# A graph layer on one core: nodes laid out 49 to a partition, and the prologue rearranged

## The reference

```python
h = maximum(layernorm(x), 0)
deg = maximum(zeros(n).at[dst].add(1.0), 1.0)
edge_weight = (deg[src] * deg[dst]) ** -0.5
edge_msg = relu(edge_attr @ W1e + b1e) @ W2e + b2e
messages = (h[src] + edge_msg) * edge_weight[:, None]
agg = segment_sum(messages, dst, n)
combined = (1.0 + gin_eps) * h + agg
out = relu(combined @ W1n + b1n) @ W2n + b2n + h
out = out * rsqrt(mean(out * out, -1) + RMS_EPS) * rms_w
return x + out
```

## Time and profile before

| | us |
|---|---|
| median of 3 runs | 1261.17 (1260.37 to 1263.86) |
| the profiled execution | 1260.41 |
| its span in the profile | 1257.8 |
| prologue, up to the first instruction of the edge pass | 0 to 122.5 |
| edge pass, up to the first instruction of the epilogue | 122.5 to 1182.5 |
| epilogue | 1182.5 to 1257.8 |

### The profile page before, as it was taken

One profiled execution on the slowest core, in us unless ns is written; L12 is line 12 of the kernel. 1 busy time (PEld: TensorE's weight loads), 2 busy tenths in 40 slices (PEclk: granted clock), 3 DMA queues, 4 the chain that ended last, 5 costly groups with the idle time before them and its releaser, 6 DMA issues. The chain is left out here.

```text
span 1257.8 us, 34843 instructions
## 1 busy us (share of the span) xinstructions
PE 1062.9 (85%) x12091; PEld 760.6 (60%) x12091; DVE 927.2 (74%) x4458; ACT 700.9 (56%) x1205; POOL 843.4 (67%) x849
## 2 busy tenths in 40 slices
PE   1041799999999999998999999999999989999475
PEld 0041477776666676666766666666676666666343
DVE  2996988787776787777867767777777678674266
ACT  1322566666565566655655656656666556565064
POOL 5221777777777777777777777777777777777012
PEclk9999999999999999999999999999999999999698
DMA  6007643533534434435435345344353353343442
GB/s 172 1 8 120 199 130 110 166 111 111 166 111 115 161 112 148 129 110 160 116 112 165 111 112 165 111 141 136 110 166 112 109 166 111 113 143 53 113 134 68
DMA packets 74824, 154.28 MB, mean 123 GB/s; under 512 B 22124, under 2 KB 48256, under 8 KB 68896
## 3 DMA queue, kind: packets, MB, share of 16 engines
q1 hardware_dynamic: 42372, 95.34, 22.2%
q0 software_dynamic: 25920, 53.55, 18.6%
q10 hardware_dynamic: 6364, 3.20, 1.0%
HBM read 145.38 MB, written 6.63 MB: 121 GB/s over the span
## 5 line engine op out<-in xcount | busy, mean ns | idle before, releaser
L863 POOL DMA_INDIRECT arena<-node_rows,arena x810 | 792.4, 978 | 267.0 <-issue 238.0
L1022 ACT ACTIVATE arena<-bank 128x686 f16<-128x686 f32 x405 | 367.9, 908 | 250.8 <-PE bank L934 250.5
L1014 ACT ACTIVATE arena<-bank 128x512 f32<-128x512 f32 (+1 forms) x450 | 245.2, 555 | 163.9 <-PE bank L889 122.4
L945 PE MATMUL bank<-t_words,arena 128*126 128x256 f16 x2205 | 299.5, 276 | 0.0
L889 PE MATMUL bank<-w1e,arena 64*128 64x128 f32 x3240 | 248.4, 273 | 0.0
L1104 DVE SCALAR_TENSOR_TENSOR arena<-iota_h,hi_f,bank 128x98 f32<-128x98 f32 x810 | 221.7, 310 | 27.0 <-PE bank L899 23.7
L945 PEld LDWEIGHTS bank<-t_words,arena 128*126 128x126 f16 x2205 | 235.3, 137 | 3.7 <-issue 2.9
L1088 DVE TENSOR_SCALAR arena<-iota_c,code 128x343 f16<-128x343 f16 x810 | 225.5, 320 | 6.1 <-PE bank L934 6.0
L889 PEld LDWEIGHTS bank<-w1e,arena 64*128 64x128 f32 x3240 | 217.6, 191 | 0.0
L1134 DVE TENSOR_TENSOR arena<-arena 128x128 f32<-128x128 f32 (+1 forms) x225 | 62.0, 275 | 172.4 <-DMA arena<-node_rows,arena 172.2
L934 PE MATMUL bank<-arena 128*128 128x343 f16 x810 | 186.2, 312 | 0.6 <-DVE arena L1088 0.2
(11 more groups left out here) (189 smaller groups left out, 882.3 us busy)
## 6 DMA issues: line engine op xcount, KB each, us to landing
arena<-in_attr SPq DMA_DIRECT2D x45, 1152.0 KB
arena<-low_src SPq DMA_DIRECT2D x45, 576.0 KB
arena<-node_rows,arena POOLq DMA_INDIRECT x810
node_rows<-arena SPq DMA_DIRECT2D x1, 3096.0 KB
out<-arena SPq DMA_DIRECT2D x12, 256.0 KB
arena<-in_x ACTq DMA_DIRECT2D x6, 448.0 KB, 12.1
arena<-node_rows SPq DMA_DIRECT2D x1, 2064.0 KB
arena<-node_rows SPq DMA_DIRECT2D x1, 1032.0 KB, 5.6
```

The costliest lines, as they stand in the source:

```text
L863: nc.gpsimd.indirect_dma_start(out=edge_rows[:, u, j, 0:ROW], out_offset=None, in_=table, in_offset=bass.IndirectOffsetOnAxis(ap=idx[:, u, ...
L945: mm = nc.tensor.matmul(x_sum[0:XC, 0:2 * D], strip[:, u, k, :], T16[:, k, :], start=k == 0, stop=k == NBLK - 1)
L1014: ins = nc.scalar.activation(out.rearrange("p (j o) d -> p o j d", o=2), of, ACT.Relu)
L1022: nc.scalar.activation(strip[:, u, :, 2 * p * W:2 * p * W + 2 * W].rearrange("p k (t w) -> p t k w", t=2), pair_bank[:, :].rearrange("p (t ...
```

## The change

Node n now sits in partition n // 49, column n % 49. `per_node` gives, for columns k0 to k1, the body (127 full partitions, in each one run of (k1 - k0) nodes' words in memory) and the rest (27 nodes in partition 127, one run). All transfers of x, `node_rows` and out use it. Parts of the node number are now made by a multiplication and a shift in DVE instead of a mask and a shift. `heads` comes by a broadcast load. Statistics of the columns 28 to 48 are taken by ACT (a sum, then a sum of squares, with accumulation) instead of by DVE. The codes are made at the end of the prologue by `encode`. In the last step only tiles with real edges are gathered. Order and waits of the prologue change with it, and ACT's copy of `acc` in the epilogue reads every 49th word.

```diff
+        def per_node(ap, k0, k1):
+            k2 = min(k1, PREST)
+            body = ap[0:PFULL * NBLK, :].rearrange("(p k) d -> p k d", k=NBLK)[:, k0:k1, :]
+            return body, ap[PFULL * NBLK + k0:PFULL * NBLK + k2, :].unsqueeze(0) if k0 < k2 else None
...
@@ sync, prologue
+                sp.dma_start(heads.bitcast(I32), t["heads"].broadcast_to((128, S * TS))).then_inc(heads_in, 16)
...
-                sp.dma_start(table[0:FULL * NB, :].rearrange("(k p) w -> p k w", p=NB), rows[:, 0:FULL, :]).then_inc(stored, 16)
-                sp.dma_start(table[FULL * NB:N, :], rows[0:REST, FULL, :]).then_inc(stored, 16)
+                body, rest = per_node(table, 0, NBLK)
+                sp.dma_start(body, rows[0:PFULL, :, :]).then_inc(stored, 16)
+                sp.dma_start(rest, rows[PFULL:PFULL + 1, 0:PREST, :]).then_inc(stored, 16)
@@ scalar, prologue
-                    act.dma_start(x_sb[:, k0:full, :], t["x"][k0 * NB:full * NB, :].rearrange("(k p) d -> p k d", p=NB)).then_inc(x_in[j], 16)
-                act.dma_start(x_sb[0:REST, FULL, :], t["x"][FULL * NB:N, :]).then_inc(x_in[-1], 16)
-                act.wait_ge(heads_ps, 1)
+                    body, rest = per_node(t["x"], k0, k1)
+                    act.dma_start(x_sb[0:PFULL, k0:k1, :], body).then_inc(x_in[j], 16)
+                    if rest is not None:
+                        act.dma_start(x_sb[PFULL:PFULL + 1, k0:min(k1, PREST), :], rest).then_inc(x_in[j], 16)
+                act.wait_ge(heads_in, 16)
+                nc.scalar.activation(heads, heads.bitcast(I32), ACT.Copy).then_inc(heads_ready, 1)
+                for j, (k0, k1) in enumerate(slices):
+                    if k0 >= halves[1][0]:
+                        act.wait_ge(x_in[j], 32 if k0 < PREST else 16)
+                        for k in range(k0, k1):
+                            ins = nc.scalar.activation(rows[:, k, 1:ROW], x_sb[:, k, :], ACT.Copy, accum_out=stat[:, 0, k:k + 1])
+                ins.then_inc(summed_x, 1)
+                act.wait_ge(mean_ready, 1)
+                for k in range(*halves[1]):
+                    ins = nc.scalar.activation(rows[:, k, 1:ROW], x_sb[:, k, :], ACT.Square, bias=stat[:, 1, k:k + 1],
+                                               accum_out=stat[:, 2, k:k + 1])
+                ins.then_inc(summed_sq, 1)
@@ vector, prologue
-                nc.vector.memset(x_sb[96:128, FULL, :], 0.0).then_inc(x_padded, 1)
+                nc.vector.memset(x_sb[96:128, PREST:NBLK, :], 0.0).then_inc(x_padded, 1)
...
                 for j in range(4):
                     statistics(j)
-                scales(*halves[0])
+                late = slice(*halves[1])
+                v.wait_ge(summed_x, 1)
+                nc.vector.tensor_scalar(stat[:, 1, late], stat[:, 0, late], -1.0 / D, None, ALU.mult).then_inc(mean_ready, 1)
                 v.wait_ge(total_ready, 1)
...
+                    pass_step(nc.vector.tensor_scalar(nid_i[:, 0, :], nid_f[:, :], float(DIV), None, ALU.mult))
+                    pass_step(nc.vector.tensor_scalar(nid_i[:, 1, :], nid_i[:, 0, :], SHIFT, None, ALU.arith_shift_right))
...
+                encode(nc, code, hi_f, rel_d, steps_of(heads[:, 0:S * TD], TD), step)
@@ epilogue
-                    nc.scalar.activation(stage[:, u, 0:n, :].rearrange("p g n -> p (g n)"), acc[:, bass.ds(e * (G * NB), n * NB)],
+                    nc.scalar.activation(stage[:, u, 0:n, :], acc[:, 0:NB * NBLK].rearrange("f (p k) -> f k p", k=NBLK)[:, cols(e), :],
...
+                for k0, k1, loaded in ((0, near, rows_in), (near, NBLK, rest_in)):
+                    body, rest = per_node(table, k0, k1)
+                    sp.dma_start(rows[0:PFULL, k0:k1, :], body).then_inc(loaded, 16)
+                    sp.dma_start(rows[PFULL:PFULL + 1, k0:min(k1, PREST), :], rest).then_inc(loaded, 16)
+                body, rest = per_node(t["x"], 0, NBLK)
+                sp.dma_start(x_sb[0:PFULL, :, :], body).then_inc(x_in, 16)
+                sp.dma_start(x_sb[PFULL:PFULL + 1, 0:PREST, :], rest).then_inc(x_in, 16)
+                body, rest = per_node(t["out"], 0, NBLK)
                 with sp.Fori(0, GROUPS - 1) as e:
                     sp.wait_ge(y_ready, e + 1)
+                    sp.dma_start(body[:, bass.ds(e * G, G), :], x_sb[0:PFULL, bass.ds(e * G, G), :]).then_inc(stored, 16)
...
+def fetched(c, i):
+    first, n = UNITS_G[i]
+    return [j for j in range(first, first + n) if (c * TS + TILE_G[j]) * 128 < E]
+
+def landings(c, u, i):
+    return sum(16 * len(fetched(b, i)) for b in range(u, c + 1, 2))
@@ gpsimd, edge pass
-                        for j in range(first, first + n):
+                        for j in fetched(c, i):
```

More of the change, by code:

```diff
@@ L33 @@
 EP = S * TS * 128
+SLOTS_D = [(g, i) for i in range(4) for g in range(4)] + [(0, 4), (1, 4)]
+SLOTS_G = [(0, 0), (1, 0)] + [(g, i + (g < 2)) for i in range(4) for g in range(4)]
+TILE_D, TILE_G = [GROUP_AT[g] + i for g, i in SLOTS_D], [TD + GROUP_AT[g] + i for g, i in SLOTS_G]
 W = 7
@@ L48 @@
 J = 2 * S
+DIV, SHIFT = 2675, 17
+assert all(n * DIV >> SHIFT == n // NBLK and n * DIV < 2 ** 24 for n in range(NB * NBLK))
 ACCW = N + 2 * WIN
@@ L360, in _ @@
-                v.wait_ge(dst_in, 16)
-                nc.vector.tensor_copy(dst_e, dst_e.bitcast(I32)).then_inc(dst_ready, 1)
-                v.wait_ge(dst_ready, 1)
+                step(nc.vector.tensor_copy(stat[:, 5, 4:5], pos_i[:, 0:1]))
+                nc.vector.scalar_tensor_tensor(out=win_pos[:, 0:1], in0=stat[:, 5, 4:5], scalar=-float(W), in1=part_f[:, :],
+                                               op0=ALU.mult, op1=ALU.add)
+                nc.vector.memset(bias_split[:, :, :], 0.0)
@@ new lines, in _ @@
+                v.wait_ge(heads_ready, 1)
+                step(nc.vector.scalar_tensor_tensor(out=rel16, in0=dst_e, scalar=-(W - 1) / 2, in1=heads, op0=ALU.add, op1=ALU.subtract))
+                nc.vector.tensor_reduce(extreme[:, 0:1], rel16, AX.X, ALU.max, apply_absolute_value=True)
+                rel_flat = rel_s[:, :, :].rearrange("p s t -> p (s t)")
+                for (out, _), (a, h) in zip(by_group(rel_flat, heads), by_group(dst_e, heads)):
+                    ins = nc.vector.tensor_tensor(out, a, h, ALU.subtract)
@@ L389, in statistics @@
                 def statistics(j):
-                    v.wait_ge(x_in[j], 16 if j < len(slices) - 1 else 32)
+                    v.wait_ge(x_in[j], 32 if slices[j][0] < PREST else 16)
                     for k in range(*slices[j]):
@@ L411, in offsets @@
                     inverse_root(root, var, a)
-                    nc.vector.scalar_tensor_tensor(out=b, in0=b, scalar=-0.5, in1=root, op0=ALU.mult, op1=ALU.mult).then_inc(scale_ready, 1)
+                    if k0 == 0:
+                        ins = nc.vector.scalar_tensor_tensor(out=b, in0=b, scalar=-0.5, in1=root, op0=ALU.mult, op1=ALU.mult)
+                    else:
+                        ins = nc.vector.tensor_tensor(b, stat[:, 1, part], root, ALU.mult)
+                    ins.then_inc(scale_ready, 1)
                 def inverse_root(root, of, a):
@@ L452, in _ @@
-                step(nc.vector.tensor_scalar(heads, heads, fast[:, 0:1], None, ALU.mult))
+                nc.vector.tensor_tensor(dst_e, dst_e, heads, ALU.subtract).then_inc(rel_ready, 1)
+                scales(*halves[0])
+                v.wait_ge(rel_ready, 1)
+                nc.vector.tensor_copy(rel_d[:, :, :], steps_of(dst_e, TS)[:, :, 0:TD]).then_inc(npass_ready, 1)
                 offsets(*halves[0])
-                for (out, _), (a, h) in zip(by_group(rel_flat, heads), by_group(dst_e, heads)):
-                    ins = nc.vector.tensor_tensor(out, a, h, ALU.subtract)
@@ L456, in _ @@
-                step(ins)
-                nc.vector.tensor_tensor(dst_e, dst_e, heads, ALU.subtract).then_inc(rel_ready, 1)
-                for j in range(4, len(slices)):
-                    statistics(j)
-                scales(*halves[1])
-                v.wait_ge(rel_ready, 1)
-                nc.vector.tensor_copy(rel_d[:, :, :], steps_of(dst_e, TS)[:, :, 0:TD])
-                offsets(*halves[1])
+                v.wait_ge(summed_sq, 1)
+                step(nc.vector.tensor_scalar(stat[:, 2, late], stat[:, 2, late], 1.0 / D, EPS_LN, ALU.mult, ALU.add))
```

202 lines of the change are left out of this document (93 added, 109 removed).

## The result

The changed kernel takes 1750.18 us (median of 4 runs, 1749.90 to 1751.44) against 1262.09 for the kernel before on the same chip: a ratio of 1.387, 95% interval 1.385 to 1.389. The forecast was 1769 us, in the range 1700 to 1840. The profiled execution took 1750.08 us, its span is 1748.1.

A forecast was written before the change was run, and what follows sets the result against it. Before: POOL's gathers bound the edge pass, a DVE chain the prologue, readback then compute the epilogue. Forecast: span 1257.8 + 201.6 - 7 + 314.1 = 1766.5, plus 2.6 around it, 1769 us; range 1700 to 1840.

The forecast's parts named there:

- The main term: Big transfers of x, `node_rows` and out: bodies of 127 partitions each use one DMA engine, at 25 GB/s; chance 0.87.
- Part 1: Prologue, load of x: one engine moves 3.38 MB in 135.1 us, so the last slice lands at 140.6.
- Part 2: Prologue, from the last x slice to `s_written`: 52.0 us, so `s_written` is at 192.6, against 101.3.
- Part 3: Store of `node_rows` before the edge pass: 130.9 us, ending at 323.5; the edge pass starts 201.6 us later.
- Part 4: Edge pass: 8 gathers less, so PE's own work sets the end; 7 us less, bounds 0 and 10.
- Part 5: Epilogue: readback, x load and thirteen stores on one engine take 389.4 us in place of 75.3, 314.1 more.
- the upper end: All one-engine transfers: the fast bound on the engine's rate, 27.1 GB/s instead of 25, giving 1719 us.
- Sixteen engines: All stages: the bodies spread over all sixteen DMA engines, so the kernel gets 36 us faster, 1224 us; chance 0.06.
- The slow single engine: All big transfers: one engine, no faster than with short pieces, 18.4 GB/s, giving 2001 us; chance 0.05.
- the hidden load: Prologue: the x load is hidden anyway, making the prologue at most 58 us shorter, 1711 us; chance 0.02.

## Why the prediction was right, and where its sizes were off

**The main term.** "127 is prime: one engine" was read from two rows over 106 partitions. It held: share 0.06 to 0.07 in four windows, and the transfers alone showed it from 127 down to 96. The three stages that it was to lengthen gave back 102, 106 and 292 us when their bodies were cut.

**Part 1**, x load: last slice at 138.9 for 140.6. The price of 25 GB/s was right here. What I didn't see is DVE's wait of 83.86 us at L398. ACT converts `heads` only after its queue has issued all x loads, and with one engine behind them the issues ended at 103.11. It is hidden only because DVE needs x until 141 anyway.

**Part 2**, last slice to `s_written`: 59.65 us for 52.0. The term was too small in three places. The start of the degree pass came 15.0 after the slice for 13.1 (ACT's squares follow one another at 0.385 us and not 0.3, and DVE waits for its root); the pass until the placing product 23.75 for 22.3, with L500 at 1.93 us where it needs 0.2; and from there to the degree 18.7 for 14.4, where L538, L540 and L542 take 2.19, 2.21 and 2.62 for 0.58, 0.58 and 1.0. All four stand beside an addition of POOL. I had counted passes by their length alone and not asked what POOL does beside them, though the trace of before has the same: its L401 and L403 on 21 elements take 1.98 and 1.93 us beside POOL's additions, and 0.2 on 28 elements without them.

**Part 3**, store: 122.9 us from the issue to the first load of the edge pass for 131.5. This is 3.21 MB at 27, not 25 GB/s. The first gather came 198.6 us later than before, for 201.6. The claim that earlier codes save nothing at POOL's pace held, and the 4.3 us that part 2 charges for them in the prologue were right too (4.4 when they were taken out).

**Part 4**, edge pass: the time from the first gather to the first read-back is 4.6 us shorter, for 7. PE's own work set the end, as forecast: PE's last unit starts 7.15 us earlier after the first gather than before. From there to the end, the units at the full clock give back 2.0 us more (5.6 us from that unit to the last addition to `acc`, before 7.6). But the encoding for the next pass also runs after the last one, 4.2 us from 1368.58, and I had not counted it: 8.8 less and 4.2 more.

**Part 5**, epilogue: 371.6 for 389.4, the largest miss. x was in after 241.9 us for 257.9, which is the rate again (6.40 MB at 26.8), and 129.7 from POOL's first addition on, at 25 GB/s as forecast. ACT's copy of every 49th word costs 1.05 us in the mean, between the bounds of 0.60 and 6, and is hidden here, as forecast; with the loads repaired it costs 2.9 us.

Sum: 3.0 less before the first gather (5.9 too little up to `s_written`, 8.6 too much in the store, 0.3 behind it), 2.4 too little in the pass, 17.8 too much in the epilogue: 18.4 less than the 1766.5 of the forecast, the 1748.1 measured. The largest mis-sized term is the rate of one engine, 25 where the store of `node_rows` and the two read-backs got 27; the upper end, 27.1, was right for these three of five transfers. Part of the closeness is luck: 8.3 us too little stand against 26.7 too much.

**The rivals.** Sixteen engines: shown false, and its own time, 1224, was also too low. With everything cut the ratio is 0.988 on the other chip. Put together from stages (first gather 9.5 earlier, pass 4.6 shorter, epilogue 2.7 longer), 1260.4 - 11.4 = 1249 us is my estimate for the first chips, 25 more than the rival. The mean comes at 39.1 for 30.5 (whose terms add up to 29.9), and IOTA's hold is 7.0 of that; from the mean to `s_written` it takes 57.4 for 49.4, with 6.6 in the four instructions beside POOL's additions; from there to the first gather 0.9 more; the pass lacks 2.4, since the encoding at its end costs 4.2; and the epilogue is 2.7 longer, not 2 shorter, with 2.9 in the copies. The slow single engine and the hidden load: both out, by the windows and by the x cut.

## What to carry over

Before transfers are laid out by partition, look at the number of partitions of the body: 127 puts everything on one engine, 106 on two, and 112 + 15 costs one more issue and repairs it. When work moves between engines, look at what POOL does beside DVE at that time, since a DVE instruction of 2 elements can then last as long as POOL's. And a part that moves out of a loop's head shows its price where it lands: find which engine is the longer side there.

## What was unexpected of the hardware

- A DVE instruction on 2 elements took 11.92 us beside a POOL IOTA of 12.08, and 0.16 without it. In the kernel before, DVE stood 14.93 us waiting for POOL's constants, which were made behind the same IOTA.
- A tensor_tensor on DVE is held by one on POOL (2.55 for 0.69 us), where POOL's IOTA and memset leave DVE's tensor_tensor alone.
- One DMA engine carries 27.2 GB/s of long rows in a load and about 23 in pieces of 512 bytes, more than the 18.4 that each of sixteen gave in such pieces.
- A queue whose transfers all go to one engine holds up its issuer: single issues of ACT lasted 18.32, 17.31 and 17.06 us, and its table load, in front of which the profile shows no wait, stood behind them until 103.11. With the bodies of x cut the table load came at 12.16.
- At the end of the pass before, the units behind PE's waits of 2.60 and 2.21 us took 1.08 us for 0.64, at a granted clock of 0.50 (1.2 GHz). So POOL's eight last gathers cost more than the waits themselves.
